# Pairing two batches in the shared network of a gated expert layer: 512 moving columns to a product

## What is computed

```
share_out  = gelu(x @ sWi0) * (x @ sWi1) @ sWo
expert_out = gelu(x @ Wi0[label]) * (x @ Wi1[label]) @ Wo[label]     # per batch
gate_in    = concat([expert_out[:, 0], share_out[:, 0]])
w          = softmax(relu(gate_in @ g0) @ g1)
return x + expert_out * w[:, 0] + share_out * w[:, 1]
```

## Time and profile before

| | |
|---|---|
| median of 3 runs | 2015.59 us (2015.51 to 2016.4) |
| the profiled execution's own time | 2016.26 us |
| its span, first to last instruction | 2014.5 us |
| PE busy | 1998.1 us (99%) |
| DVE busy | 1633.1 us (81%) |
| ACT busy | 1197.0 us (59%) |
| DMA | 230.88 MB, mean 115 GB/s |

### The profile page before, as it was taken

How to read it: one execution, slowest core, us unless ns; L and a number is a source line. 1 busy time by engine, 2 the same in 40 slices (tenths; PEclk the granted TensorE clock), 3 DMA queues, 4 the chain that set the end, 5 groups by cost and what they waited for, 6 DMA issues and landing times.

```text
span 2014.5 us, 34984 instructions
## 1 busy us (share of the span) xinstructions
PE 1998.1 (99%) x13846; PEld 1869.9 (93%) x13846; DVE 1633.1 (81%) x1914; ACT 1197.0 (59%) x1658; POOL 82.2 (4%) x56
## 2 busy tenths in 40 slices
PE   9999999999999999999999999999999999999997
PEld 7999999999999999999999999999999999999997
DVE  7778788787887878878788788887888878888776
ACT  6555566555666556665666556656565665656653
POOL 0001000010000100001000010000100001000000
PEclk9999999999999999999999999999999999999999
DMA  4444333433334333343243442334423343233431
GB/s 157 137 132 126 99 95 110 147 121 94 100 116 142 116 95 116 105 137 117 94 125 96 136 134 77 126 95 151 127 80 115 104 153 121 88 106 120 137 95 42
DMA packets 188021, 230.88 MB, mean 115 GB/s; under 512 B 13266, under 2 KB 152530, under 8 KB 185810
## 3 DMA queue, kind: packets, MB, share of 16 engines
q1 hardware_dynamic: 187858, 228.65, 35.8%
HBM read 220.21 MB, written 8.39 MB: 113 GB/s over the span
## 4 chain that ended last, share of the span: by engine, by line
PE 93%; DVE 4%; ACT 1%; issue 1%; DMA 0%; SPq 0%; POOL 0%; DVEq 0%; POOLq 0%; ACTq 0%
PE ps_pv L273 35%; PE ps_out L282 33%; PE ps_c L273 26%; DVE al L544 2%; DVE gate_prod L709 1%; DVE act L674 0%; DMA a_src<-shared 0%; ACT ah L383 0%; DVE wo0l L544 0%; ACT hidh L414 0%; SPq L187 0%; DVE act L668 0%; DVE act L670 0%; DVE a_src L561 0%; ACT ps_pv L481 0%
## 5 line engine op out<-in xcount | busy, mean ns | idle before, releaser
L544 DVE TENSOR_TENSOR al<-a_src,ah 128x512 fp32r<-128x512 f32 (+2 forms) x385 | 546.7, 1420 | 104.9 <-ACT ah L383 100.2
L273 PE MATMUL ps_pv<-xh,al 128*128 128x256 f32 x2048 | 580.2, 283 | 0.8 <-ACT ps_pv L481 0.6
L273 PE MATMUL ps_pv<-xl,ah 128*128 128x256 f32 x2048 | 579.5, 283 | 0.0
L273 PE MATMUL ps_pv<-xh,ah 128*128 128x256 f32 x2048 | 579.5, 283 | 0.0
L383 ACT CAST ah<-a_src 128x2048 fp32r<-128x2048 f32 x381 | 453.6, 1191 | 3.3 <-DVE a_src L561 3.3
L273 PE MATMUL ps_c<-xh,al 128*128 128x256 f32 x1540 | 435.6, 283 | 2.8 <-DVE xl L544 2.0
L273 PE MATMUL ps_c<-xh,ah 128*128 128x256 f32 x1540 | 435.8, 283 | 0.0
L273 PE MATMUL ps_c<-xl,ah 128*128 128x256 f32 x1540 | 435.8, 283 | 0.0
L273 PEld LDWEIGHTS ps_pv<-xh,al 128*128 128x128 f32 x2048 | 393.1, 192 | 2.0 <-issue 1.7
L273 PEld LDWEIGHTS ps_pv<-xh,ah 128*128 128x128 f32 x2048 | 393.1, 192 | 0.0
L273 PEld LDWEIGHTS ps_pv<-xl,ah 128*128 128x128 f32 x2048 | 393.1, 192 | 0.0
(11 more groups left out here) (74 smaller groups left out, 2418.2 us busy)
## 6 DMA issues: line engine op xcount, KB each, us to landing
a_src<-shared SPq DMA_DIRECT2D x256, 256.0 KB, 4.0
a_src<-experts SPq DMA_DIRECT2D x256, 256.0 KB, 3.9
raw_wo<-shared SPq DMA_DIRECT2D x128, 256.0 KB, 2.9
raw_wo<-experts SPq DMA_DIRECT2D x128, 256.0 KB, 2.8
x_src<-x_cols SPq DMA_DIRECT2D x32, 256.0 KB, 4.7
x_res<-x_rows SPq DMA_DIRECT2D x8, 1024.0 KB, 9.0
out<-s_out SPq DMA_DIRECT2D x7, 1024.0 KB, 6.3
g_sb<-g_rows SPq DMA_DIRECT2D x1, 2048.0 KB, 8.6
```

The lines of the kernel that those rows point to most:

```text
L273: mm = nc.tensor.matmul(ps[:, a * HALF:(a + 1) * HALF], a_op[ap][:, i, a, k, :], x_op[xp][:, j, k, :], start=(start and a == 0 and k == 0 ...
L544: nc.vector.tensor_tensor(to, of, hi.bitcast(F32), ALU.subtract).then_inc(done, 1)
```

## The change

Two batches (2p, 2p+1) make a pair. The order is now: expert pass of batch 2p (8 steps), shared pass for both batches (8 steps), expert pass of batch 2p+1 (8 steps). A pair's two shared passes of 8 steps are now one: there are 96 steps in place of 128, and a shared ("wide") step has two turns, a gate turn (t even within it) and a linear turn. The moving operand `x_op` holds both batches, and one block product of a turn is 6 matmuls of 512 columns, 256 of each batch, for the gate columns or for the linear columns alone; it fills a whole bank.

Per wide step, the weights are loaded, summed and split once for the two batches; the hidden layer is split for both at once (`hs` with 2048 columns); the down tiles of the first batch stand in the gate turn and those of the second in the linear turn. Since four banks can't hold two batches' sums, each shared down tile is a complete group, and DVE adds it into `s_out` in SBUF (`add_tile`; the first step's tiles are copied). The linear turn of the first wide step has no down tiles; the 8 tiles of the last one stand in the first step of the next expert pass. `x_lo`, gate and mix are moved to other steps, the gate's weights are loaded in halves when they are needed (`g0_sb` is shared with `x_res`), the label of batch 0 is loaded and read before the first weights, and the last batch's rows are loaded into freed buffers.

```diff
-            for b in range(BATCH):
-                one_pass(b, SHARED, b * (2 * STEPS), b == 0, False)
-                one_pass(b, EXPERT, b * (2 * STEPS) + STEPS, False, b == BATCH - 1)
+            for pair in range(PAIRS):
+                n0 = pair * PAIR_STEPS
+                expert_pass(2 * pair, n0)
+                shared_pass(2 * pair, n0 + STEPS)
+                expert_pass(2 * pair + 1, n0 + 2 * STEPS)
...
+            def wide_product(i, a, ps, start):
+                for k in range(2):
+                    for q, (ap, xp) in enumerate(PASSES):
+                        mm = nc.tensor.matmul(ps, a_op[ap][:, i, a, k, :],
+                                              x_op[xp][:, i, k, :, :].rearrange("p h t -> p (h t)"),
+                                              start=(start and k == 0 and q == 0), stop=(k == 1 and q == 2),
...
+            def shared_turn(n, c, b, a):
+                t = first_turn(n) + a
+                if a == GATE:
+                    pe.wait_ge(a_ready, a_splits(n, 0))
...
+                c11_taken(t - 1)
+                wide_product(P1, a, ps_c11[:, :], True).then_inc(p_done[P1], 1)
+                pe.wait_ge(c12_done, t - 1)
+                wide_product(P5, a, ps_p5, True).then_inc(p_done[P5], 1)
+                pe.wait_ge(p1_copied, t)
+                wide_product(P6, a, ps_v, False).then_inc(p_done[P6], 1)
+                wide_product(P2, a, ps_c11[:, :], False).then_inc(p_done[P2], 1)
...
+                pe.wait_ge(v_copied, t)
+                wide_product(P7, a, ps_v, False).then_inc(p_done[P7], 1)
+                wide_product(P3, a, ps_p5, False).then_inc(p_done[P3], 1)
...
+                for m in range(MC):
+                    if c > 0:
+                        shared_tile(m, a, b, n - 1)
+                    elif a == GATE:
+                        expert_tile(m, b, n - 1)
...
+                pe.wait_ge(u_copied, t)
+                wide_product(P4, a, ps_c21[:, :], False).then_inc(p_done[P4], 1)
...
+            def shared_gate(n, c, b):          # on ACT
+                t = first_turn(n)
+                c21_gelu(t - 1)
+                copy_p1(t)
+                hid_hi(n - 1)
+                save_p5(t)
+                copy_v(t)
+                a_hi(n, 2)
...
+                gelu(act[:, :, 0, 0:HALF], halves(ps_c11[:, :]))
+                copy_u(t)
...
+                gelu(act[:, :, :, HALF:TOK], act[:, :, :, HALF:TOK])
+                wo_hi(n)
+                if c == 0:
+                    copies_out(b, t)
...
+            def shared_lin(n):                 # on ACT
+                t = last_turn(n)
+                c21_gelu(t - 1)
+                copy_p1(t)
+                save_p5(t)
+                copy_v(t)
+                copy_u(t)
+                a_hi(n + 1, 0)
+                a_hi(n + 1, 1)
...
+            def shared_gate(n, c, b):          # on DVE
+                c21_product(t - 1)
+                weight_sums(n + 1, 0)
+                weight_sums(n + 1, 1)
+                hid_lo(n - 1)
+                weight_sums(n + 1, 2)
+                a_lo(n, 2)
...
+                c22(t, act[:, :, 1, HALF:TOK])
+                c12(t, act[:, :, 0, HALF:TOK])
+                if c > 0:
+                    for m in range(MC):
+                        add_tile(m, 0, b, n - 1, t, 0)
+                wo_lo(n)
...
+            def shared_lin(n, c, b):           # on DVE
+                t = last_turn(n)
+                c11_product(t)
...
+                c22(t, lin[:, :, 1, :])
+                c12(t, lin[:, :, 0, :])
...
+                nc.vector.tensor_tensor(act[:, :, :, HALF:TOK], act[:, :, :, HALF:TOK], lin[:, :, :, :], ALU.mult
+                                        ).then_inc(product_done, 1)
+                a_lo(n + 1, 0)
+                if c > 0:
+                    for m in range(MC):
+                        add_tile(m, 1, b, n - 1, t, 0)
+                a_lo(n + 1, 1)
...
+                if n % STEPS == 0:             # add_tile
...
+                    nc.vector.tensor_copy(to, ps_out[m][:, :]).then_inc(added, 1)
+                else:
...
+                    nc.vector.tensor_tensor(to, to, ps_out[m][:, :], ALU.add).then_inc(added, 1)
```

More of the change, by code:

```diff
@@ L37, with first_turn, is_wide, last_turn @@
 PASSES = [(LO, HI), (HI, LO), (HI, HI)]
+STEPS = 8
+PAIR_STEPS = 3 * STEPS
+PAIR_TURNS = 4 * STEPS
+WIDE0 = STEPS
+EXPERT1 = 3 * STEPS
+def first_turn(n):
+    pair, q = divmod(n, PAIR_STEPS)
+    return pair * PAIR_TURNS + (q if q < STEPS else 2 * q - STEPS if q < 2 * STEPS else q + STEPS)
+def is_wide(n):
+    return STEPS <= n % PAIR_STEPS < 2 * STEPS
+def last_turn(n):
+    return first_turn(n) + (1 if is_wide(n) else 0)
+def down_turn(n):
+    return last_turn(n + 1) if is_wide(n) else first_turn(n + 1)
+def is_gate(t):
+    q = t % PAIR_TURNS
+    return WIDE0 <= q < EXPERT1 and q % 2 == 0
+def is_lin(t):
+    q = t % PAIR_TURNS
+    return WIDE0 <= q < EXPERT1 and q % 2 == 1
+def downs(t):
+    return 4 * t - (4 if WIDE0 < t % PAIR_TURNS < EXPERT1 else 0)
+def gelus(t):
+    pair, q = divmod(t, PAIR_TURNS)
+    wide = min(max(q - WIDE0, 0), 2 * STEPS)
+    return 3 * (pair * PAIR_STEPS + q - wide + (wide + 1) // 2)
+def products(t):
+    pair, q = divmod(t, PAIR_TURNS)
+    wide = min(max(q - WIDE0, 0), 2 * STEPS)
+    return 3 * (pair * PAIR_STEPS + q - wide + wide // 2)
 def a_splits(m, g):
@@ L226, in one_pass, with next_wo, expert_pass @@
+            def next_wo(n):
+                if n + 1 < N_STEPS:
+                    sp.wait_ge(wo_ready, n + 1)
+                    load_wo(n + 1)
+            def expert_pass(b, n0):
+                last = b == BATCH - 1
+                if b == 0:
                     first_loads()
-                if net == SHARED:
-                    sp.wait_ge(labels_loaded, 16)
-                label = sp.value_load(labels_sb[0:1, bass.ds(b, 1)], min_val=0, max_val=N_EXPERTS - 1)
+                elif b % 2 == 1 and not last:
+                    read_label(b + 1)
@@ L230, in one_pass @@
                 for c in range(STEPS):
[L231 to L245, removed]
@@ L261, in _, with shared_pass @@
+                    if c == 6 and last:
+                        sp.wait_ge(gate_prod_done, b * 2 * NC + NC)
+                        load_gate(EXPERT)
+                        load_last_rows()
+                    next_wo(n0 + c)
+            def shared_pass(b, n0):
+                read_label(b + 1)
+                for c in range(STEPS):
+                    next_a(n0 + c)
+                    next_wo(n0 + c)
+            schedule(expert_pass, shared_pass)
             for m in range(MC):
                 sp.wait_ge(last_mixed, m + 1)
-                sp.dma_start(out[BATCH - 1, :, m, :], s_out[:, m, :]).then_inc(out_stored, 16)
+                sp.dma_start(out[BATCH - 1, :, m, :], s_out[:, 1, m, :]).then_inc(out_stored, 16)
@@ L279, in down @@
[L279 to L283, removed]
+                                                  x_op[xp][:, j, k, h, :],
+                                                  start=(start and a == 0 and k == 0 and q == 0),
@@ L284, in down @@
                                               skip_group_check=True)
                 return mm
+            def down(m, s, start, stop, hidden):
+                for f in range(2):
+                    for q, (hp, wp) in enumerate(PASSES):
+                        mm = nc.tensor.matmul(ps_out[m][:, :], hidden[hp][:, f, m * P:(m + 1) * P], wo[s][wp][:, f, :],
+                                              start=(start and f == 0 and q == 0), stop=(stop and f == 1 and q == 2),
+                                              skip_group_check=True)
+                return mm
@@ L306, in step, with c11_taken, expert_tile @@
-            def step(n, c, b, net, first, last):
+                product(P4, P2, 0, ps_c21, False).then_inc(direct_done, 1)
+                product(P7, P7, 0, ps_v, True)
+                product(P4, P3, 0, ps_v, False).then_inc(direct_done, 1)
+            def c11_taken(t):
+                if is_gate(t):
+                    pe.wait_ge(gelu_done, gelus(t) + 1)
+                else:
+                    pe.wait_ge(product_done, products(t) + 1)
+            def expert_tile(m, b, n):
+                c = n % STEPS
+                if c == 0 and b % 2 == 1:
+                    pe.wait_ge(added, (b // 2 + 1) * PAIR_ADDS - MC + (m + 1))
+                elif c == 0 and b > 0:
+                    pe.wait_ge(out_copied, (b - 1) * MC + (m + 1))
+                down(m, n % 2, c == 0, c == STEPS - 1, hidden_of[0]).then_inc(down_done, 1)
@@ L483, in step @@
                     hid_hi(0)
[L484 to L485 removed]
+                    wo_hi(0)
+                a_hi(n, 2)
                 if n == 1:
                     first_x_hi(P4)
[L488 to L493 removed]
@@ L507, in step @@
-                if new_x:
-                    x_hi(b + 1, 1, n)
-                wo_hi(n, s)
-                if not first and c == 0:
```

(46 more changed lines are left out.)

599 lines of the change are left out of this document (370 added, 229 removed).

## The result

The changed kernel takes 1995.4 us, the median of four runs (1992.22 to 1998.23), against 2015.55 for the kernel before beside it: ratio 0.9899, interval 0.9881 to 0.9917, so 20 us or 1.0% faster. Run once more, on the chip that ran *late1*, *late3* and *split1i*, it took 1994.57 (1992.99 to 1996.2), ratio 0.9892 (0.9877 to 0.9907); the other four experiments ran on another chip, where the kernel before took 2016.11 and not 2015.75, so a difference between the two sets is sure to some 0.4 us only. The forecast was 1993. The profiled execution took 1992.22 us, span 1990.4.

A forecast was written before the change was run, and what follows sets the result against it. Between start and tail only PE's rate counts. Wide matmuls -37.1, first-linear-turn wait +12.2 and start +2 sum to -22.9 us, from 2016.26 to 1993.4 profiled, 1993 (1992.7) for the median; range 1981 to 2006.

The forecast's parts named there:

- Wide matmuls: In 32 wide steps, 132 matmuls of 512 columns at 0.2267 us take 29.92 instead of 31.08: -37.1 us.
- the estimate of 7 us: For wide matmuls, the skill's columns / 2.4 + 2.5 ns gives a 7 us gain; set aside for the measured rows.
- The wait in the first linear turn: Without down tiles there, PE waits 3.05 us for `a_lo` group 0, once in each of four pairs: +12.2 us.
- The clock: Rival: the four 3 us waits lower PE's clock to 1.2 GHz, losing 2.2 us each, 9 in all: 2002; chance 0.11.
- a clock of 1.00 throughout: Sign in the new trace that PE keeps full clock; a fall after a wait would show the prediction wrong.
- Start: At the kernel's start, waiting for the label before any weights makes the last weights' issue later: +2 us.
- The adds: On DVE, 8 per wide step, 256 in all, 0.69 us each; linear turn's C21 product starts at T+0.35, T being P5's start.
- The cover before P7: In gate turns, `hid_hi` of 2048 columns precedes two PSUM copies on ACT; 0.85 us of lateness is covered, costing nothing.
- Its ACT part: 0.3 us by which the C21 product comes before ACT is free for `hid_hi`.
- The part up to P7: Slack of 0.53 us between the `ps_v` copy's end at T+3.55 and P7, due at T+4.08.
- Expert steps, gate, loads: In expert steps, PE's work is unchanged and moved DVE work, gate halves and loads stay covered: no cost.

The follow-up runs named there:

- late1: Changed kernel with one scratch 128x512 SBUF add on DVE behind the four tile adds of 28 linear turns; 2001.53 us, ratio 0.9931.
- late3: Changed kernel with three scratch 128x512 SBUF adds on DVE behind the four tile adds of 28 linear turns; 2042.77 us, ratio 1.0133.
- split1i: Changed kernel with three expert down tiles moved into each pair's first linear turn and 18 instead of 10 zero matmuls at the start; 1978.24 us, ratio 0.9813.
- halves: Changed kernel with each wide matmul split into two of 256 columns, the same weights loaded twice; 2033.28 us, ratio 1.0082.
- again: The changed kernel itself, unaltered, run once more; 1994.57 us, ratio 0.9892.

## Why the prediction was right, point by point

- **Wide matmuls, -37.1:** right. 0.2267 each, 29.92 a step, and *halves* gives it back (37 by its turns, 38.7 measured). The same rows contradict the estimate of 7 us from the Trainium skill's formula, which its section gives for the gap of an isolated matmul.
- **The wait in the first linear turn, +12.2:** right in place, cause and size. 2.94 each in the list of waits, 3.24 in the length of the turn (13.0 in all), as the first matmul after a wait starts later than without one.
- **The clock:** given as a rival with 0.11 and left out of the sum. It came true in part: it fell at one or two of four waits in the two profiled runs, and cost 1.5 to 2.8 us each where 2.2 was put. By the prediction's own list a fall after a wait is a sign of being wrong, and a clock of 1.00 throughout was to be seen; on this point the mechanism was wrong, at a price of 1.5 and 4.3 us. That it would be neither always nor never was not foreseen.
- **Start, +2:** the size was near, the mechanism in part another. In the first profile the first copy of P1 begins at 22.49 where it began at 21.85, +0.6: the sums of the second step's weights start at 14.32 and not 13.68, while the DMA engines are busy all the time (share 0.98 from 8 to 12 us). In *again* it is +1.9, by the slow first matmuls, which the prediction doesn't have; over the nine profiles of the changed kernel and its variants it lies between +0.6 and +2.6.
- **The adds:** 0.684 and 0.686 against 0.69. C21's product ran from 311.64 to 312.32, T+0.4 (P5 begins at 311.94), against T+0.35.
- **The cover before P7:** named as the tightest, but mis-sized, 0.85 where late1 gives 0.48. Its ACT part was 0.3 as put. The part up to P7, put at 0.53, was hardly 0.1: the copy of `ps_v` ended at T+3.74, 0.19 later than put, and the weights' load must wait too. It cost nothing in this kernel.
- **Expert steps, gate, loads:** nothing, as said, though the slack that it was read from is 2.9 us and not 3.1 (1043.01 - 1040.13). Steps that take 15.54 are still 15.54. Seven steps of the kernel before that took 15.91 (five) or 15.65 (two) are gone, 2.1 us that the forecast didn't count. Each comes where a gate half stands in DVE's queue and POOL makes the differences of the next x, in that step or the one behind it, and there DVE's rows are longer than elsewhere: 3.22 in place of 2.29, 2.31 in place of 1.22. That POOL's work is what slows them is likely, but no run tests it. In four of the seven P7 then waits for the copy of `ps_v`:

```profile
170.68 8.22 POOL L774 TENSOR_TENSOR x_src<-x_src 128x512 f32<-128x512 f32 x4 [25.04 <-DMA x_src<-x_cols]
172.82 3.22 DVE L544 TENSOR_TENSOR al<-a_src,ah 128x2048 fp32r<-128x2048 f32 x1
```
```profile
PE ps_pv L273 <- ACT ps_pv L481: 0.6, 4, 0.2
```

The ledger of the first profiled run, from spans: -37.1 for the wide steps, +13.0 for the waits, +1.5 for one fall, +0.6 at the start, -2.1 for the lost small waits: -24.1. The spans differ by 2014.5 - 1990.4 = 24.1. For *again* it is -37.1 + 13.0 + 4.3 + 1.9 - 2.1 = -20.0, and the spans differ by 20.1. The forecast's -22.9 lies between the two. That it came so near is in part luck: it missed 2.1 us of gain and 1.5 to 4.3 us of loss by the clock, and these worked against each other.

## What to carry to other kernels

When PE is the bound, look at the time from one matmul's start to the next in both widths. A fixed part per matmul is paid per instruction, so twice the columns on the same weights saves it once each time, whatever else the pairing does. When work is moved off a turn, see what it covered: here four down tiles hid a chain of copy, split and sum, and three of them moved back were worth as much as 80% of the gain (16.0 against 20). And count a cover (the time by which work may be late before PE waits) down to the weights' load, not to the matmul.

## What the runs showed of the hardware

- A semaphore wait ahead of a matmul shows as a delay of its weights' load: 0.12 us after the copy's end in both kernels, with the matmul 0.22 behind when all is in time. The delays in late1 (up to 0.25 in each of 24 turns, 5.6 us) are in no row of waits of PE, but in one of PEld.
- At the same wait of 2.94 us the granted clock fell to 0.50 in some places and not in others: at one of the four places in the first profile, at two in *again* and *late1*, at three in *late3*. At waits of 7.2 us it fell in four of four. A fall cost 1.5 to 2.8 us, and filling the wait with idle matmuls bought back 3 to 4 us of 1995.
- The first products start 0.21 apart, the rate of 1.2 GHz, for some 12 matmuls in the profile of *late1*, 16 in the changed kernel's first and 25 in *again*. That, and the time of the first loads, moves the first copy of P1 by 2.0 us between profiles (22.49 to 24.48).
- A float32r matmul took 0.120 us with 256 columns and 0.2267 with 512, that is 0.013 above its columns at 2.4 GHz in both cases.
